# Up products and gated values moved to the last slot of a batch, and the stage between two layers dealt in small parts

## The reference

```
x = x + L0_xattn(layernorm(x), ctx)     # 16 heads, causal
x = x + L0_ffn(layernorm(x))            # 8 experts, top 1, and one shared expert
x = x + L1_xattn(layernorm(x), ctx)     # latent attention, 16 heads, rotary, all 1444 keys
x = x + L1_ffn(layernorm(x))            # ternary weights, 8 bit activations, silu(gate) * up, rms norm, down
```

## Time and profile before

| | us |
|---|---|
| median of 3 runs | 933.36 (930.14 to 933.48) |
| the profiled execution | 933.26 |
| its span, first to last instruction | 931.5 |
| TensorE busy in the span | 834.7 (90%) |
| VectorE / ScalarE / GpSimd busy | 576.2 / 397.2 / 451.6 |

### The profile page before, as it was taken

The page is one execution under the profiler, slowest core; times in us unless marked ns, Lnnn a source line. Parts: engine busy times, 40 slices in busy tenths (PEclk is TensorE's granted clock), DMA queues, the critical chain, the costliest instruction groups (busy, mean ns, idle before and its releaser), DMA issues.

```text
span 931.5 us, 15596 instructions
## 1 busy us (share of the span) xinstructions
PE 834.7 (90%) x5844; PEld 615.6 (66%) x5844; DVE 576.2 (62%) x1133; ACT 397.2 (43%) x882; POOL 451.6 (48%) x465
## 2 busy tenths in 40 slices
PE   4998879989987799999899899999989989989984
PEld 3666656889865577767676676676766767765542
DVE  3537854322365576577777768768757777776445
ACT  2248851222113154544444464454354444445431
POOL 3000004700050077877686766767767766566630
PEclk8779997999998699999999999999999999999987
DMA  9541024699510000000000010000000000000000
GB/s 209 178 144 62 2 65 157 219 338 318 190 48 18 17 1 1 27 10 2 25 10 1 11 30 1 10 22 10 10 22 9 2 15 10 2 13 12 1 13 10
DMA packets 42168, 52.28 MB, mean 56 GB/s; under 512 B 12230, under 2 KB 35704, under 8 KB 41836
## 3 DMA queue, kind: packets, MB, share of 16 engines
q1 hardware_dynamic: 41068, 49.63, 17.1%
q0 software_dynamic: 1024, 1.64, 0.6%
HBM read 45.80 MB, written 5.36 MB: 55 GB/s over the span
## 4 chain that ended last, share of the span: by engine, by line
PE 68%; DVE 15%; ACT 6%; issue 5%; DMA 4%; SPq 1%; POOL 0%; POOLq 0%; DVEq 0%; ACTq 0%
PE ps L1168 13%; PE ps L1180 10%; PE ps L1148 7%; PE ps L1092 6%; PE ps L1016 4%; PE ps L1119 3%; PE ps L1097 3%; PE ps L1203 3%; PE ps L970 3%; DMA xs<-xs_scratch 2%; ACT sm L1426 2%; DVE nm L1935 2%; PE ps L1029 2%; DVE xyz L1906 2%; DVE xyz L1902 1%
## 5 line engine op out<-in xcount | busy, mean ns | idle before, releaser
L593 POOL TENSOR_TENSOR acc<-acc,pt 120x800 f32<-120x800 f32 (+1 forms) x157 | 303.6, 1934 | 98.6 <-ACT pt L1635 66.5
L1635 ACT ACTIVATE pt<-ps 120x400 f32<-120x400 f32 (+1 forms) x384 | 189.5, 504 | 226.2 <-PE ps L1168 214.9
L1935 DVE TENSOR_REDUCE nm<-ps 128x1 f32<-128x482 f32 (+1 forms) x336 | 214.3, 654 | 108.4 <-PE ps L1148 105.4
L1168 PE MATMUL ps<-qh,khl 128*120 128x400 f32 (+1 forms) x384 | 158.1, 412 | 6.6 <-ACT pt L1635 6.1
L1180 PE MATMUL ps<-pt,kv 120*64 120x400 f32 (+1 forms) x768 | 143.9, 511 | 0.0
L1148 PE MATMUL ps<-khl,qh 128*128 128x482 f32 (+1 forms) x336 | 133.9, 401 | 10.5 <-DVE nm L1935 9.0
L1168 PE MATMUL ps<-ql,kh 65*120 65x400 f32 (+1 forms) x384 | 133.3, 347 | 0.0
L1168 PEld LDWEIGHTS ps<-qh,khl 128*120 128x120 f32 (+1 forms) x384 | 70.2, 183 | 52.2 <-issue 29.6
L1180 PEld LDWEIGHTS ps<-pt,kv 120*64 120x64 f32 (+1 forms) x768 | 52.2, 139 | 66.1 <-issue 56.6
L615 POOL TENSOR_TENSOR rstd<-veps,mhalf 100x1 f32<-100x1 f32 (+2 forms) x19 | 13.0, 682 | 164.1 <-DVE veps L1769 115.3
L593 POOL TENSOR_TENSOR acc<-pt,pt 121x800 f32<-121x800 f32 x16 | 30.5, 1907 | 95.1 <-ACT pt L1635 95.1
(11 more groups left out here) (276 smaller groups left out, 1225.2 us busy)
## 6 DMA issues: line engine op xcount, KB each, us to landing
egu<-_L_ffn_gate_up_proj_dram SPq DMA_DIRECT2D x14, 1024.0 KB, 6.0
edn<-in_L_ffn_down_proj_dram SPq DMA_DIRECT2D x14, 512.0 KB, 6.9
spread<-inv_scratch SPq DMA_DIRECT2D x30, 100.0 KB, 2.8
craw<-in_ctx_dram SPq DMA_DIRECT2D x8, 360.0 KB
wo_n<-in_L_xattn_Wo_dram SPq DMA_DIRECT2D x1, 2048.0 KB, 10.4
wq_n<-in_L_xattn_Wq_dram SPq DMA_DIRECT2D x1, 2048.0 KB, 8.0
xs_scratch<-zero SPq DMA_DIRECT2D x1, 1792.0 KB, 9.8
xs<-xs_scratch SPq DMA_DIRECT2D x14, 128.0 KB, 6.1
```

The costliest lines, as they stand in the source:

```text
L593: nc.gpsimd.tensor_tensor(total[r, :, :], before[r, :, :], pt[j % PT_BUF][r, :, :], ALU.add).then_inc(p_added, 1)
L1168: last = mm(ps[0:key_rows(t), k % 2, 0:HT], lhs[:, keys], rhs[:, HT * a:HT * a + HT], start=first, stop=not first)
L1635: nc.scalar.activation(pt[j % PT_BUF][0:rows, k % 2, :], ps[0:rows, k % 2, 0:HT], ACT.Exp).then_inc(p_ready, 1)
L1935: nc.vector.tensor_reduce(nm3[0:w, i, n:n + 1], ps[0:w, 3 + m % 2, 0:MN], AX.X, ALU.max).then_inc(m_reduced, 1)
```

## The change

It has two parts in one diff.

1. The up products and the gated value go to slot 47 (`GU_SLOT = (40, 47, 47)`, `HIDDEN_SLOT = (47, 47)`), the gate stays at slot 40. The up halves use banks 4 and 3 instead of 5. On TensorE they come behind `turn_max`, the first half waiting for `max_ready`, the second for `m_kept` (ScalarE's `keep_max`). On VectorE both `hidden` halves and then `max_h` are at slot 47. The maxima of the next odd unit wait for `h1_part`.
2. The stage between the layers: `shared_out` is dealt one by one between the key turns, the query products and the maxima. `q_big(0, 1)` uses banks 0 and 1, so it need not wait for the first rope. `q_big(1, 1)`, the first four `turn_ternary`, and the four heads of `q_latent(1)` are dealt one per maxima part. `low_keys` comes before the residuals on VectorE. `third_input` of batches 5 to 7 goes to slots 2 to 4 of the big loop. A first small exponent on ScalarE is put ahead of the copies. `place_max(0)` comes before the transfer of `lnw_b` on SP. To let this overlap, several buffers lie elsewhere.

```diff
+TERNARY_AT, SECOND_AT, SECOND_ROPE_AT, LATENT_AT = (10, 11, 14, 19), (4, 5, 6, 7, 8, 9), 11, (15, 16, 17, 18)
+X2_LATE, X2_DONE, PT_LATE = (2, 3, 4), 9, 2 * 7
-GU_SLOT, TANH_SLOT, HIDDEN_SLOT = (40, 41, 43), 41, (42, 44)
+GU_SLOT, TANH_SLOT, HIDDEN_SLOT = (40, 47, 47), 41, (47, 47)
-FIRST = 3
+FIRST = 2
+def q_bank(u, a):
+    return 0 if (u, a) == (0, 1) else 6
+def shared_bank(b):
+    return 2 if b == B - 1 else 2 + b % 2
...
 def up(b, half):                                   # TensorE
-                if b == B - 2:
-                    pe.wait_ge(m_kept, NU)
-                elif half:
-                    pe.wait_ge(h1_part, 2 * b + 1)
+                if half or b == B - 2:
+                    pe.wait_ge(m_kept, min(PAIRS * (b + 2) + 1, NU))
                 else:
-                    pe.wait_ge(x3_kept, min(b + 4, B))
-                    if b:
-                        pe.wait_ge(y_ready, b)
+                    pe.wait_ge(max_ready, PAIRS * (b + 2) + 1)
 def max_chunk(u, c):                               # TensorE
+                    if p and b >= 2:
+                        pe.wait_ge(h1_part, 2 * (b - 1))
...
             turn_keys(0, 0)
+            shared_out(0)
+            shared_out(1)
+            turn_keys(0, 1)
+            shared_out(2)
+            turn_keys(0, 2)
+            shared_out(3)
             turn_x3(0)
+            pe.wait_ge(ys_kept, NT)
             for part in range(6):
                 q_big(0, 0, part)
-            turn_ternary(0)
-            turn_ternary(1)
-            turn_keys(0, 1)
             for part in range(6):
                 q_big(0, 1, part)
-            turn_ternary(2)
-            turn_ternary(3)
-            turn_keys(0, 2)
-            turn_ternary(4)
-            turn_ternary(5)
+            shared_out(4)
             q_latent(0)
-            for part in range(6):
-                q_big(1, 0, part)
-            pe.wait_ge(tails_set, 2)
-            pe.wait_ge(fq_kept, 6)
+            shared_out(5)
+            pe.wait_ge(x_shared, 6)
             for c in range(MC):
                 max_chunk(0, c)
-                if c == MC // 2:
+                if c == 1:
                     for part in range(6):
-                        q_big(1, 1, part)
+                        q_big(1, 0, part)
+                if c == 3:
+                    shared_out(6)
+                if c in SECOND_AT:
+                    q_big(1, 1, SECOND_AT.index(c))
+                if c in TERNARY_AT:
+                    turn_ternary(TERNARY_AT.index(c))
+                if c == SECOND_ROPE_AT + 2:
+                    shared_out(7)
+                if c in LATENT_AT:
+                    q_latent(1, (LATENT_AT.index(c),))
+            turn_max(0)
             turn_x3(1)
-            turn_max(0)
-            q_latent(1)
+            for n in range(len(TERNARY_AT), 6):
+                turn_ternary(n)
+            pe.wait_ge(tails_set, 3)
+            pe.wait_ge(fq_kept, 6)
...
+            nc.scalar.activation(ssq[:, 1:2], mhalf[0:S, 0:1], ACT.Exp)     # ScalarE
+            for j in range(3):
+                keep_keys(0, j)
             keep_x3(0)
+            keep_q(0)
+            for n in range(3):
+                keep_ternary(n)
+            keep_q(1)
             keep_ternary(3)
+            keep_max(0)
+            keep_x3(1)
             keep_ternary(4)
             keep_ternary(5)
...
+            low_keys(0, 0)                                                  # VectorE
+            second_residual(0)
+            second_residual(1)
+            low_keys(0, 1)
+            second_residual(2)
+            third_input(0)
+            low_keys(0, 2)
+            norm_x3(0)
+            second_residual(3)
+            third_input(1)
+            third_input(2)
+            third_input(3)
             rope(0, 0)
             rope(0, 1)
+            second_residual(4)
+            norm_x3(1)
+            third_input(4)
+            second_residual(5)
             for c in range(MC):
+                reduce_max(0, c)
                 if c == 1:
+                    low_q(0)
                     rope(1, 0)
+                    second_residual(6)
+                if c == SECOND_ROPE_AT:
                     rope(1, 1)
+                    second_residual(7)
```

More of the change, by code:

```diff
@@ L685, in _ @@
                         add_weights(pool, PSLOTS * b + s // 2)
+                    if b == 0 and s == X2_DONE:
+                        pool.wait_ge(var3_ready, B)
+                        power(rstd[:, 2:B], veps[:, 2:B], S).then_inc(rstd3_ready, 1)
+                        pool.wait_ge(rstd3_ready, 3)
                     if b >= 2 and s == H_NORM_SLOT:
@@ L1042, in _ @@
             expert_out(NT - 1)
-            for b in range(B):
-                shared_out(b)
             def turn_ternary(n):
@@ L1100, in q_big, with q_latent @@
                         last.then_inc(qbig_done, 1)
-            def q_latent(u):
+            def q_latent(u, heads=range(HG)):
                 b, p = u // PAIRS, u % PAIRS
@@ L1113, in q_latent @@
                     pe.wait_ge(x3_kept, min(b + 2, B))
-                    if b >= 2:
-                        pe.wait_ge(h1_part, 2 * (b - 1))
-                for i in range(HG):
+                    if b >= 3:
+                        pe.wait_ge(y_ready, b - 2)
+                for i in heads:
                     for j in range(3):
@@ L1313, in _ @@
                         ffn_down(b - 2)
[L1314 to L1315 removed]
+                    if b and s == ffn_slots(b, GU_SLOT, LAST_GU_SLOT)[0]:
+                        gate(b - 1)
                     if b == B - 1 and s == LAST_HQ_SLOT:
@@ L1321, in _ @@
                         turn_max(u + 1)
+                    for half in range(2):
+                        if b and s == ffn_slots(b, GU_SLOT, LAST_GU_SLOT)[1 + half]:
+                            up(b - 1, half)
                     if x == PHASE - 1:
@@ L2057, in _ @@
                         low_q(u + 1)
+                    if b == 0 and s in X2_LATE:
+                        third_input(5 + X2_LATE.index(s))
                     if u + 1 < NU and MAX_FROM <= at < MAX_FROM + MC:
@@ L2075, in _ @@
                         quantise_x(b - 1)
-                    if 1 <= b < B - 1 and s == MAX_H_SLOT:
-                        max_h(b - 1)
                     if b >= 2 and s in QH_SLOT:
@@ L2081, in _ @@
                         result(b - 2)
-                    if b and s in ffn_slots(b, HIDDEN_SLOT, LAST_HIDDEN_SLOT):
-                        hidden(b - 1, ffn_slots(b, HIDDEN_SLOT, LAST_HIDDEN_SLOT).index(s))
+                    for half in range(2):
+                        if b and s == ffn_slots(b, HIDDEN_SLOT, LAST_HIDDEN_SLOT)[half]:
+                            hidden(b - 1, half)
+                    if 1 <= b < B - 1 and s == MAX_H_SLOT:
+                        max_h(b - 1)
                     if b == B - 1 and s == LAST_HN_SLOT:
```

140 lines of the change are left out of this document (63 added, 77 removed).

## The result

The changed kernel takes 905.93 us (median of 4 runs, 900.78 to 907.98) against 933.42 (median of 4 runs, 930.14 to 934.7) of the kernel before on the same chip: a ratio of 0.970, 95% interval 0.965 to 0.975. Predicted were 908 and a range of 901 to 918. The profiled execution took 904.72 with a span of 903.0.

The account below looks back on a forecast made before the run. TensorE was taken to bound the loop, so only its idle time could be saved. Part 1's 15.0 and part 2's 10.4 us sum to 25.4, taking 933.26 to 907.9, predicted 908, range 901 to 918.

Parts of the forecast that it names:

- part 1: Up and gated value at slot 47: removes TensorE waits of 9.3 and 7.8 us, adds 2.1; saves 15.0 us.
- part 2: Stage between the layers, walked with new lists: slot 2 starts 13.4 us earlier, less 3 for the clock, 10.4 us.
- The term of 2.1: Slot 47: the second up half waits for `keep_max`, 0.35 us in each of six batches, paid in full.
- VectorE's block at slot 47: Two `hidden` halves and `max_h`, 5.4 us, covered by `q_latent` and the values, over before `low_q` can start; cost 0.
- the walk: Stage's new lists stepped through with profiled durations: first scores at 310.6, slot 2 at 313.1 against 326.48.
- The clock: Stage: low-clock falls at the longest of three idle stretches and one other with one half; 3 us, bounds 0 and 7.
- `third_input` in slots 2 to 4: Three `third_input`, 3.9 us, moved into VectorE's idle time in the loop; priced at 0, at most 1.5 us.
- The table load: Early exponent's 1.28 us load ahead of the first key copy, covered by shared products 0 and 1.
- Rival 1: Stage handoffs and clock falls give back the gain: stage gains 2 to 6, time 912 to 917 us; chance 0.12.
- Rival 2: Up half trades waits: `keep_max` late or VectorE's block reaches slot 2; part 1 gives 5 to 9, 913 to 918; chance 0.08.
- Rival 3: VectorE's slot 47 work delays `low_q` and the next unit's first reduce: slower, 938 to 945 us; chance 0.03.
- Rival 4: No effect, TensorE's waits only move to the next late thing: 930 to 936 us; chance 0.03.

Follow-up runs that it names:

- experiment 3: Changed kernel with the tanh of five batches cut to 16 of 512 columns per half, output not the reference's: 900.24 us, ratio 0.965; batch 3 72.53 against 73.31.
- experiment 4: Changed kernel with the tanh computed in two halves, after the exponents of slots 41 and 43: 897.67 us, ratio 0.961; batch 3 72.83 against 73.31.
- experiment 10: Changed kernel with the tanh of batches 1 to 6 moved to slot 47 behind `keep_max`: 903.49 us, ratio 0.975; batch 3 72.86 against 73.31.
- experiment 6: Changed kernel with the second up half behind `q_latent` instead of ahead of it: 901.50 us, ratio 0.969; batch 3 73.36 against 73.31.
- experiment 5: Changed kernel with nine useless small matmuls before TensorE's wait for the maxima: 905.29 us, ratio 0.974; last expert copy to slot 4 54.9 against 58.0.
- experiment 7: Changed kernel with `third_input` of batches 5 to 7 back in the stage: 911.43 us, ratio 0.981; last expert copy to slot 4 62.0 against 58.0.
- experiment 9: Changed kernel without the early small exponent ahead of ScalarE's copies: 908.70 us, ratio 0.980; last expert copy to slot 4 57.1 against 58.0.
- experiment 8: Changed kernel with query product, three ternary turns and `q_latent(1)` in whole pieces: 911.80 us, ratio 0.981; last expert copy to slot 4 62.9 against 58.0.

## Why the prediction was right, and where it was not

The forecast of 907.9 came 3 us from the profiled 904.72. Two terms were mis-sized in opposite directions: part 1 was 3.2 us too much (15.0, measured 11.8) and part 2 with its clock 3.4 too little (10.4, measured 13.8). The 25.4 us of the forecast stand against 25.2 measured for the change (11.8 + 13.8 - 0.4), and that they agree so closely is luck. The 3 us that remain are nobody's doing: 1.7 lie ahead of the stage and 1.6 are the fall of the clock in batch 4 of the kernel before.

- **Part 1, 9.3 + 7.8 - 2.1 = 15.0, measured 11.8** (1.96 a batch, not 2.5; the batch is 73.3 us, not 72.7). Both waits went, as the step says, 1.55 and 1.30 us in a batch, 2.85 together. What the sum lacks is a term of 6 x 0.54 = 3.2 us. TensorE's wait of 1.55 us had also been the time in which ScalarE caught up after its tanh of 1.1 us: in the kernel before it stood idle for 2.08 us ahead of the exponents at 529.44, after the change for 0.32 ahead of those at 510.26. With the wait gone, the exponents of slots 42 and 43 are late and 0.54 us returns at slot 44. Experiments 3, 4 and 10 show this: cut, split or moved, the tanh gives back 0.78, 0.48 and (in batch 1) 0.76 us. I had looked at what VectorE was relieved of in slots 41 to 44, not at what ScalarE still had there.
- **The term of 2.1 came out right for a reason that the prediction does not give.** It was to be the wait for `keep_max`, 0.35 us a batch, with up products that cost the same at slot 47. The wait is there (0.54 us ahead of the second half's weight load, part of it beside the first half's products), but experiment 6 shows that it costs nothing. The up products are what costs more. From the scores of slot 40 to the turn are 9.55 us before (522.96 to 532.51) and 6.44 after (505.54 to 511.98); without the waits named above 0.80 us of difference is left, the price of the up products between the scores. From the turn to `q_latent` are 0.21 us before and 1.35 after, 1.14 more. So they are 0.34 us dearer at slot 47, 2.0 in six batches. Why is not shown. The balance closes: 2.85 - 0.54 - 0.34 = 1.97 us a batch, and 1.96 were measured.
- **VectorE's block at slot 47, priced at 5.4 us and covered.** It lasts 6.8 us (511.85 to 518.62), because the product L2044 takes 2.40 us instead of 1.22. The step that `max_h` is over before `low_q` can start is wrong: `low_q` begins at 518.65, some 0.9 us later than ScalarE's copies allow, and the first reduce begins 1.61 us behind the first scores, where it was 1.32 before (537.62 to 538.94). The cost was 0 as predicted only because the next slots take up these 0.3 us: the exponent of slot 4 is 3.91 us behind the first in both. Experiment 10 makes the reduce another 0.8 us later and pays 0.3 us a batch.
- **Part 2, 13.4 to slot 2, measured 15.2.** Slot 2 starts at 309.55, 53.8 us behind the last expert copy, against 69.1 before, even with two slots at the low clock. The first scores come 50.4 us behind the copy, where the walk had 53.2, and slots 0 and 1 take 3.4 us at the low clock, where it had 2.5. The walk has the idle stretches in the right order and behind the right partners, down to `keep_q(1)` and one ternary copy ahead of `keep_max`; it was too dear by small amounts at these stretches (1.38 and 1.17 us measured, 1.75 and 1.6 priced), at the start of the maxima (22.9 us behind the copy, 24.8 priced) and at SP's transfer (2.94 us from the end of `keep_max` at 303.19 to the scores, 3.4 priced).
- **The clock, priced at 3 us.** One low stretch of 6.8 us, behind the longest of the three idle stretches, the one for which the prediction was surest; experiment 5 prices it at 3.1 us up to slot 4 and at 2.6 up to batch 1. So this term was right in size, and the 3.4 us that part 2 was short of lie in the walk. The shorter two brought no fall. The rule of the Trainium skill, TensorE: Matmul & The Clock Gate, section "HAM oscillation — how this bites in real kernels", that waits between bursts put the array back to the low clock, bears out at the longest wait (2.34 us) and not at those of 1.38 and 1.17. The page's own example has waits of about 3 to 5 us for a transfer; that the rule reaches stretches as short as these was the prediction's reading of it. Taken at its full cost it would have made the stage's gain 7.4 us; 13.8 were measured.
- **`third_input` in slots 2 to 4, priced at 0.** From slot 4 to slot 47 of batch 0 are 54.91 us after and 54.89 before. It is free beside the low clock of these slots; with the full clock (experiment 5) 0.5 us of it shows. Experiment 7 shows what the move is worth: 4.0 us, the clock's part included.
- **The table load.** The load was covered where the prediction had it, but it would have been covered anyway (experiment 9). The Trainium skill, ScalarE: Activation LUTs, section "What ACT_TABLE_LOAD costs", gives a drain of about the load's length behind it; no such thing is to be seen here. The first key copy starts 1.80 us after the last expert copy with the early exponent and 0.42 without, a difference of 1.38: the load of 1.28 and the exponent. In the kernel before, the load stands between two instructions of ScalarE (324.63, 1.28 us) and the first exponent follows it at 325.93.
- **The rivals.** Rival 1 fell: the small parts do not give back the gain, they are 4.9 us of it, a low stretch of 3.4 us that came with the whole pieces included (experiment 8). Rival 2 fell at `keep_max` (experiment 6), though a trade of one wait for another did take place, at slot 44. Rival 3's mechanism, VectorE's block holding up `low_q` and the first reduce, did set in, but 0.3 us of it cost TensorE nothing. Rival 4 fell with both tables above.

## What to carry to other kernels

A wait that is taken away can have paid for something else: before pricing its removal, list for every engine what it catches up on during the wait, and price what of it turns up later. A piece of work that is moved is to be priced at the new place too (here 1.14 us for 0.80). When work is gathered into one block on an engine, the block's cover is to be checked with the durations that hold beside the other engines' work at that place, not with those of the old place. An idle stretch of TensorE before the start of a loop costs its own length and, if the clock falls, about as much again (2.3 us idle, 1.6 to 3.1 us at the low clock here); filling it with products of no use saves the second part, not the first.

## What the runs showed of the hardware

- **VectorE and GpSimd take turns, and the one that starts second stands.** The product of two operands from SBUF (L2003 before, L2044 after) takes 1.22 us in the kernel before. The groups by line over the loop (count, busy us, mean ns, idle before), before:

```profile
L2003 DVE TENSOR_TENSOR sg<-h,lnw_b 100x1024 f32<-100x1024 f32 x6 | 7.3, 1216 | 0.0
```

  and after:

```profile
L2044 DVE TENSOR_TENSOR sg<-h,lnw_b 100x1024 f32<-100x1024 f32 x6 | 14.1, 2346 | 0.2
```

  It lay beside GpSimd's adds before the change as well. There it began first (532.37), and the add that began 0.27 us later took 2.71 us instead of the usual 1.88, so GpSimd paid:

```profile
532.64 2.71 POOL L593 TENSOR_TENSOR acc<-acc,pt 120x800 f32<-120x800 f32 x1
```

  After the change it begins at 514.96, while the last of four adds runs, which end at 516.28, and now it is the product that grows: 1.18 us are added in the 1.3 us that they lie side by side. With the tanh at slot 47 it begins 0.4 us before the adds end and takes 1.50. GpSimd's next small product begins at 516.23, before L2044 ends, and takes 1.45 us where it took 0.46. So the move to slot 47 did not bring the two together, it turned round who waits. The Trainium skill, GPSIMD Engine Reference, section "1. Specifications", names contention of GpSimd with VectorE's instructions that have two SBUF inputs; the trace agrees, and gives its price. `reduce_max` (655 ns on average in the earlier trace rows and still 655 over the whole kernel after), which reads one operand, from PSUM, is not affected.
- **Which wait lets the clock fall is not settled by its length.** In the changed kernel 2.34 us did and 1.38 didn't. With the third inputs in the stage (experiment 7) TensorE waited 2.96 us at 289.10 and kept the full clock, and after 2.57 us at 299.83 it fell from 301.4 for 6.8 us. With whole pieces (experiment 8) it fell at 294.6 for 3.4 us with no wait above 0.53 us in the 7 us before it. The same wait of 2.3 us before the first scores was followed by 6.8 us of low clock in some profiles and 3.4 in others (copy to slot 4: 58.0 and 56.5, and 57.1 where it began 2 us earlier). What decides this stays open.
